# Attention with its causal masks on VectorE and GpSimd instead of TensorE, and two key steps per group

## What is computed

```
q, k, v = (h @ Wqkv + bqkv) split, 16 heads of 32, 1024 positions, 4 batches
scores = q k / sqrt(32), by key and query; masked where key > query (-10000)
attn = softmax(scores over the keys)
x = x + ga * ((attn applied to v) @ Wo + bo)
```

## Time and profile before

| | |
|---|---|
| median of 3 runs | 2444.23 us (2442.47 to 2448.04) |
| span of the profiled execution | 2451.0 us |
| TensorE busy | 2043.9 us (83%) |
| VectorE busy | 1115.6 us (46%) |
| ScalarE busy | 763.2 us (31%) |
| GpSimd busy | 510.1 us (21%) |
| attention, all four batches | about 60 to 1490 us |

### The profile page before, as it was taken

How to read it: one execution, slowest core, us unless ns; L and a number is a source line. 1 busy time by engine, 2 the same in 40 slices (tenths; PEclk the granted TensorE clock), 3 DMA queues, 4 the chain that set the end, 5 groups by cost and what they waited for, 6 DMA issues and landing times. The chain is left out here.

```text
span 2451.0 us, 34688 instructions
## 1 busy us (share of the span) xinstructions
PE 2043.9 (83%) x10812; PEld 1248.9 (51%) x10813; DVE 1115.6 (46%) x2207; ACT 763.2 (31%) x1215; POOL 510.1 (21%) x491
## 2 busy tenths in 40 slices
PE   4899997899987889987998995899999939999900
PEld 1644543654444545434544532676776726666600
DVE  3434553354444345443444435555665323333358
ACT  1244452344452244452244442122221102222200
POOL 0200005100006000006000014444555421000064
PEclk8899998899998899998899997999999969999955
DMA  6212213211213221213222114222222168333388
GB/s 215 52 27 52 44 44 105 52 38 41 52 35 105 52 52 37 42 35 104 52 52 52 32 41 182 71 93 82 90 90 95 65 231 282 127 127 128 116 280 320
DMA packets 104965, 232.49 MB, mean 95 GB/s; under 512 B 20440, under 2 KB 20440, under 8 KB 104812
## 3 DMA queue, kind: packets, MB, share of 16 engines
q1 hardware_dynamic: 81008, 171.86, 24.4%
q0 software_dynamic: 14848, 50.34, 5.7%
q10 hardware_dynamic: 8960, 8.41, 1.2%
HBM read 113.06 MB, written 67.17 MB: 74 GB/s over the span
## 5 line engine op out<-in xcount | busy, mean ns | idle before, releaser
L459 DVE TENSOR_REDUCE mx<-ring 128x1 f32<-128x512 f32 (+3 forms) x640 | 369.4, 632 | 395.6 <-PE ring L569 305.0
L367 ACT ACTIVATE pr<-sc 128x1024 f32<-128x1024 f32 (+3 forms) x384 | 307.9, 810 | 416.3 <-PE sc L601 343.2
L617 PE MATMUL O<-pr,V 128*32 128x512 f32 (+3 forms) x3072 | 343.0, 524 | 34.7 <-ACT pr L367 29.5
L598 PE MATMUL sc<-stk 128*128 128x512 f32 (+3 forms) x768 | 271.0, 427 | 42.4 <-ACT stk L356 42.4
L598 PEld LDWEIGHTS sc<-stk 128*128 128x128 f32 x768 | 144.2, 200 | 292.2 <-issue 189.4
L322 POOL TENSOR_TENSOR oT<-oV,oD 128x512 f32<-128x512 f32 x32 | 41.0, 1282 | 1165.8 <-DVE oD L481 1165.8
L569 PE MATMUL ring<-stk 96*128 96x512 f32 (+3 forms) x768 | 258.7, 434 | 27.4 <-DMA stk<-st 26.9
L569 PEld LDWEIGHTS ring<-stk 96*128 96x128 f32 x768 | 154.8, 215 | 38.8 <-issue 16.4
L1475 PE MATMUL ue<-wu_e,xT_e 128*128 x632 | 151.2, 383 | 0.1
L1489 PE MATMUL de<-wd_e,aT_e 128*128 x316 | 148.5, 593 | 0.0
L481 DVE RECIPROCAL oD<-oD 128x512 f32<-128x512 f32 x32 | 105.5, 3330 | 88.5 <-ACT oD L379 88.5
(11 more groups left out here) (233 smaller groups left out, 3478.3 us busy)
## 6 DMA issues: line engine op xcount, KB each, us to landing
stk<-st SPq DMA_DIRECT2D x192, 256.0 KB, 5.0
x_e<-xs SPq DMA_DIRECT2D x79, 256.0 KB, 2.6
ys<-y_e SPq DMA_DIRECT2D x79, 256.0 KB, 2.0
oT<-in_L_attn_x_dram ACTq DMA_DIRECT2D x16, 512.0 KB, 5.7
xr<-in_L_attn_x_dram SPq DMA_DIRECT2D x32, 256.0 KB, 2.8
x1d<-h SPq DMA_DIRECT2D x32, 256.0 KB, 2.0
xb<-x1d SPq DMA_DIRECT2D x32, 256.0 KB, 3.1
part<-y_sh SPq DMA_DIRECT2D x32, 256.0 KB, 2.0
```

The lines of the kernel that those rows point to most:

```text
L367: nc.scalar.activation(pr[:, g % 3, :, off:], sc[g % 2][:, :, off:], ACT.Exp, scale=SCALE).then_inc(exp_done, 1)
L459: nc.vector.tensor_reduce(mx[:, heads[0]:heads[-1] + 1, qt, part], bank[:, 0:len(heads) * w].rearrange("p (e k) -> p e k", e=len(heads)), ...
L598: last = nc.tensor.matmul(sc[g % 2][:, e, off:], K.stk[:, p % 2, 1, e, i * P:(i + 1) * P], K.stk[:, p % 2, 0, e, c * CH + off:(c + 1) * CH ...
L617: last = nc.tensor.matmul(O[row:row + 32, off:], V[:, col:col + DH], pr[:, g % 3, e, off:], start=(i == 0), stop=(i == 4 * c + 3))
```

## The change

It takes both mask matmuls off TensorE. For the maxima, VectorE's `tensor_tensor_reduce` adds a mask (0 or -1e30, `K.mask`, 128 x 512 of f32, of which the last columns are used) to the product, writes the sum back to PSUM and reduces it by maximum; it takes one head at a time, so that 16 such instructions replace 12 of the 20 reductions of a pair, and 8 stay. For the scores the exponentials above the diagonal are set to zero by an `affine_select` on GpSimd (`upper_off`, two heads of 128 columns at once, 8 per pair), for which the weighted sums of these steps then wait.

The key steps run in six groups of two. `M_GROUP` gives the maxima tasks before, between and after the two scores of each group. The weighted sums of a group come together after the scores of the next one; those of steps 10 and 11 come after `m_transpose` of the next pair. There are four buffers `pr`. On ScalarE the copy of the second chunk comes after `mt_evac`. On VectorE both reciprocals of a head group come in the next even pair, after that pair's first reduction, and the POOL multiplications follow in the same pair. SyncE starts the DMAs of `stk` at the end of the scores of the pair two before, not of its weighted sums, and `ga_bc`, `gabo_bc` and `xr` share memory with `st` and are loaded after the last `stk`. The set-up ends with a clearing of its semaphores and a barrier of all engines, and makes fewer constants.

The core of the diff:

```diff
...
-M_FROM, M_RATE = 4, 3
+    nc.clear_and_free_semaphores(held)
+    nc.all_engine_barrier()
...
+M_GROUP = ((0, 0, 1), (2, 2, 1), (2, 2, 1), (2, 2, 1), (2, 2, 0), (0, 0, 0))
+PRB = 4
...
+
+        late = st[:, 0:2, :].bitcast(f32).rearrange("p a s -> p (a s)")
+        ga_bc, gabo_bc = late[:, 0:D], late[:, D:2 * D]
+        xr = late[:, 2 * D:4 * D].rearrange("p (j d) -> p j d", d=D)
         V, S_t = K.V, K.S
...
         mhi = sb("mhi", [P, NT, 2], f32r)
-        pr = sb("pr", [P, 3, 2, CH])
+        pr = sb("pr", [P, PRB, 2, CH])
...
             with sp.Fori(0, NB) as b:
-                sp.wait_ge(u_ready, b * NT + PRIMED)
-                sp.dma_start(ga_bc[:, :], K.modd[bass.ds(b, 1), GA, :].broadcast_to([P, D])).then_inc(mod2_in, 16)
-                sp.wait_ge(x1_ready, b * NT + PRIMED)
-                sp.dma_start(gabo_bc[:, :], K.modd[bass.ds(b, 1), GABO, :].broadcast_to([P, D])).then_inc(mod2_in, 16)
                 for p in range(NPAIR):
                     if p >= 2:
-                        sp.wait_ge(pv_done, b * (NPAIR * NST) + NST * (p - 1) + PRIMED)
+                        sp.wait_ge(sc_done, b * (NPAIR * NST) + NST * (p - 1))
                         apart(sp)
...
                                 .then_inc(stk_in[p % 2], 16)
+                for s in range(2):
+                    sp.wait_ge(stk_in[s], (b * NHG + NHG) * STACKED + PRIMED)
+                sp.dma_start(ga_bc[:, :], K.modd[bass.ds(b, 1), GA, :].broadcast_to([P, D])).then_inc(mod2_in, 16)
+                sp.dma_start(gabo_bc[:, :], K.modd[bass.ds(b, 1), GABO, :].broadcast_to([P, D])).then_inc(mod2_in, 16)
                 for j in range(NT):
-                    if j < 2:
-                        sp.wait_ge(x1_ready, b * NT + PRIMED)
-                    else:
+                    if j >= 2:
                         sp.wait_ge(x1_ready, b * NT + j - 1 + PRIMED)
...
+
+            def upper_off(b, p, s):
+
+                c, i = STEPS[s]
+                off = i * P - c * CH
+                g = p * NST + s
+                pool.wait_ge(exp_done, b * NPAIR * NST + g + 1 + PRIMED)
+                apart(pool)
+                t = pr[:, g % PRB, :, off:off + P]
+                nc.gpsimd.affine_select(out=t, in_=t, compare_op=ALU.is_ge, fill=0.0, base=0,
+                                        pattern=[[0, 2], [1, P]], channel_multiplier=-1).then_inc(tri_done, 1)
+
+            def normalise(b, n):
+                hg, c = n // 2, CHUNKS[n % 2]
+                pool.wait_ge(o_rec, b * 8 + n + 1)
+                nc.gpsimd.tensor_tensor(oT[:, hg, c * CH:(c + 1) * CH], oV[:, c, :], oD[:, c, :], ALU.mult).then_inc(o_norm, 1)
...
                 split_low(b, NT - 1)
-                for n in range(2 * NHG):
-                    hg, c = n // 2, CHUNKS[n % 2]
-                    pool.wait_ge(o_rec, b * 8 + n + 1)
-                    nc.gpsimd.tensor_tensor(oT[:, hg, c * CH:(c + 1) * CH], oV[:, c, :], oD[:, c, :], ALU.mult).then_inc(o_norm, 1)
+                for p in range(NPAIR):
+                    for s in DIAG:
+                        upper_off(b, p, s)
+                        if p % 2 == 0 and p >= 2 and s in (DIAG[1], DIAG[3]):
+                            normalise(b, p - 2 + DIAG.index(s) // 2)
+                    if p == NPAIR - 1:
+                        normalise(b, p - 1)
+                        normalise(b, p)
                 pool.wait_ge(mod2_in, b * 32 + 32)
...
-                if p >= 2:
-                    act.wait_ge(pv_done, b * NPAIR * NST + NST * (p - 1) + PRIMED)
...
                 act.wait_ge(sc_done, b * NPAIR * NST + g + 1)
-                if g >= 3:
-                    act.wait_ge(pv_done, b * NPAIR * NST + g - 2 + PRIMED)
-                nc.scalar.activation(pr[:, g % 3, :, off:], sc[g % 2][:, :, off:], ACT.Exp, scale=SCALE).then_inc(exp_done, 1)
+                if g >= PRB:
+                    act.wait_ge(pv_done, b * NPAIR * NST + g - PRB + 1 + PRIMED)
+                nc.scalar.activation(pr[:, g % PRB, :, off:], sc[g % 2][:, :, off:], ACT.Exp, scale=SCALE).then_inc(exp_done, 1)
...
                         exp(b, p, s)
-                        if s == TURN:
+                        if s == TURN + 1:
                             o_copy(b, 2 * p)
-                    o_copy(b, 2 * p + 1)
                     if p % 2 == 0 and p + 2 < NPAIR:
...
                         mt_evac(b, p + 1)
+                    o_copy(b, 2 * p + 1)
...
                 dve.wait_ge(m_done, b * NPAIR * NM + p * NM + n + 1)
-                nc.vector.tensor_reduce(mx[:, heads[0]:heads[-1] + 1, qt, part],
-                                        bank[:, 0:len(heads) * w].rearrange("p (e k) -> p e k", e=len(heads)),
-                                        AX.X, ALU.max).then_inc(m_red, 1)
+                if k0 <= qt * P < k0 + w:
+                    apart(dve)
+                    for x_, e in enumerate(heads):
+                        o = bank[:, x_ * w:(x_ + 1) * w]
+                        last = nc.vector.tensor_tensor_reduce(out=o, in0=o, in1=K.mask[:, CH - w:CH], scale=1.0, scalar=MASKED,
+                                                              op0=ALU.add, op1=ALU.max, accum_out=mx[:, e, qt, part:part + 1])
+                    last.then_inc(m_red, 1)
+                else:
+                    nc.vector.tensor_reduce(mx[:, heads[0]:heads[-1] + 1, qt, part],
+                                            bank[:, 0:len(heads) * w].rearrange("p (e k) -> p e k", e=len(heads)),
+                                            AX.X, ALU.max).then_inc(m_red, 1)
...
                 for p in range(NPAIR):
-                    n = 0
-                    for s in range(NST + 1):
-                        if p + 1 < NPAIR:
-                            while n < M_DUE[s]:
-                                m_reduce(b, p + 1, n)
-                                n += 1
-                        if s == TURN + 1 and p == NPAIR - 1:
-                            o_recip(b, p - 1)
                     if p + 1 < NPAIR:
+                        for n in range(NM):
+                            m_reduce(b, p + 1, n)
+                            if n == sum(M_GROUP[0]) - 1 and p % 2 == 0 and p >= 2:
+                                o_recip(b, p - 2)
+                                o_recip(b, p - 1)
                         m_rows(b, p + 1)
...
                         p_low(b, (p + 2) // 2)
-                    if p % 2:
-                        if p < NPAIR - 1:
-                            o_recip(b, p - 1)
-                        o_recip(b, p)
+                o_recip(b, NPAIR - 2)
+                o_recip(b, NPAIR - 1)
                 dve.wait_ge(mod2_in, b * 32 + 32)
...
                 bank = bank_for(b, "m", NM * p + n)
-                diag = k0 <= qt * P < k0 + w
                 for x_, e in enumerate(heads):
-                    o = bank[:, x_ * w:(x_ + 1) * w]
-                    last = nc.tensor.matmul(o, K.stk[0:96, p % 2, 0, e, qt * P:(qt + 1) * P], K.stk[0:96, p % 2, 1, e, k0:k0 + w],
-                                            start=True, stop=not diag)
-                    if diag:
-                        last = nc.tensor.matmul(o[:, qt * P - k0:qt * P - k0 + P], K.identb[:, :], K.mask_qk[:, :],
-                                                start=False, stop=True)
+                    last = nc.tensor.matmul(bank[:, x_ * w:(x_ + 1) * w], K.stk[0:96, p % 2, 0, e, qt * P:(qt + 1) * P],
+                                            K.stk[0:96, p % 2, 1, e, k0:k0 + w], start=True, stop=True)
                 last.then_inc(m_done, 1)
...
                 pe.wait_ge(mt_ready, b * 16 + 2 * p + CHUNKS.index(c) + 1)
-                diag = i * P >= c * CH
                 for e in range(2):
                     last = nc.tensor.matmul(sc[g % 2][:, e, off:], K.stk[:, p % 2, 1, e, i * P:(i + 1) * P],
-                                            K.stk[:, p % 2, 0, e, c * CH + off:(c + 1) * CH], start=True, stop=not diag)
-                    if diag:
-                        last = nc.tensor.matmul(sc[g % 2][:, e, off:off + P], K.identb[:, :], K.mask_kq[:, :], start=False, stop=True)
+                                            K.stk[:, p % 2, 0, e, c * CH + off:(c + 1) * CH], start=True, stop=True)
                 last.then_inc(sc_done, 1)
...
                     pe.wait_ge(o_copied, b * 16 + n + PRIMED)
-                pe.wait_ge(exp_done, b * NPAIR * NST + g + 1 + PRIMED)
+                if s in DIAG:
+                    pe.wait_ge(tri_done, b * NPAIR * ND + p * ND + DIAG.index(s) + 1)
+                else:
+                    pe.wait_ge(exp_done, b * NPAIR * NST + g + 1 + PRIMED)
                 for e in range(2):
...
                         row = 64 * z + 32 * e
-                        last = nc.tensor.matmul(O[row:row + 32, off:], V[:, col:col + DH], pr[:, g % 3, e, off:],
+                        last = nc.tensor.matmul(O[row:row + 32, off:], V[:, col:col + DH], pr[:, g % PRB, e, off:],
```

(32 more changed lines are left out.)

36 lines of the change are left out of this document (18 added, 18 removed).

## The result

The changed kernel takes 2542.99 us (median of 4 runs, 2540.82 to 2545.02), the kernel before in the same set 2443.35 us: a ratio of 1.0402, 95% interval 1.0378 to 1.0425. That is 100 us slower. Forecast were 2525 us, 81 slower, in a range of 2420 to 2600. The profiled execution has a span of 2539.1 us against 2451.0, 88 us more: the profiled execution of the kernel before is longer than its median, that of the changed one shorter.

The account below looks back on a forecast made before the run. TensorE's in-order list was taken to set the length. A batch: +3.0 - 5.3 + 3 x 1.7 + 3 x 6.15 - 1.3 = +20.0 us; four batches and the barrier +81, so 2525 us, range 2420 to 2600.

Parts of the forecast that it names:

- The first wait: TensorE's first maxima matmul of a pair waits for the DMAs into stk: 8.3 us in odd, 5 in even pairs.
- The second: In pairs 2, 4 and 6 TensorE's task 4 waits 7.1 us for a ring bank while VectorE does both reciprocals.
- an odd pair: Length of an odd pair, with the wait for stk and 2.0 us for the clock: 31.0 us against 29.3, +1.7.
- an even pair: Length of an even pair from 2 on, without projection, with both waits: 33.85 us against 27.7, +6.15.
- pair 7: Last pair of a batch, with no maxima to prepare: about 21.7 us against 23.0, -1.3.
- TensorE's own list: TensorE's work and short waits from a pair's first maxima task to the next m_transpose: 17.3 us, with maxima matmuls 4.5.
- x: Extra time of each tensor_tensor_reduce on VectorE for handing over its scalar result: 0 to 0.168 us, taken as 0.1.
- Rival A: VectorE becomes the bound because the new instruction runs at half rate or its result costs much: about 2620 us; chance 0.1.
- The clock: Idling of 7 to 8 us drops TensorE to 1.2 GHz: 2.0 us for each of six pairs a batch.
- B: The reciprocals' wait doesn't hurt, so 7.1 us drop out of 12 pairs: 2440 us; chance 0.14.
- C: Neither wait stands, the copies land before they are asked for: about 2250 us, or 2350 with half the waits; chance 0.1.
- D: The masks' matmuls were hidden, so TensorE's list is 3.4 us longer in each pair: about 2630 us; chance 0.04.

Follow-up runs that it names:

- late tasks: Changed kernel with later M_GROUP, first maxima task behind scores 2, 3 and weighted sums 0, 1: 1.0097 alone, 0.9715 with reciprocals before the pair's first maximum.
- the projection first: Changed kernel with reciprocals before the first maximum and the next projection moved from the end of even pairs to behind scores 0 and 1: 0.9713; 0.9519 with later M_GROUP.
- the wait filled: Changed kernel with reciprocals before the first maximum, plus matmuls nobody reads (34 in odd, 17 in even pairs from 2) in TensorE's wait for stk: 2426.68 us, 0.9905.
- masks back: Changed kernel with its new order kept but both masks again matmuls on TensorE, plain reductions and no select: 2619.04 us, 1.0686.
- the kernel with the reciprocals first: Changed kernel with VectorE's two reciprocals before instead of after the first maximum in even pairs from 2 on: 2457.89 us, 1.0009.

## Why the prediction was right, point by point

**The first wait** was forecast as 8.3 us in odd pairs and 5 in even ones, from the 10.0 us of the copy and what is left to do meanwhile. Measured: 8.26 and 4.51, and from `m_transpose` to the landing 11.67 us (157.00 to 168.67) where I had 11.7. That this wait costs what it seems to is shown by the kernels with late tasks and with the projection first: the loss goes when something else covers the copy or starts it earlier.

**The second** was forecast as 7.1 us, with TensorE at task 4 again 8.55 us after the landing. It got there 8.50 us after it (205.15 - 196.65). The bare wait was 5.67, less than 7.1, because the work of 1.4 us ahead of it ran at half clock and took 2.8 (8.50 less 5.67). Moving the reciprocals took 96 us away.

**The terms of a batch**, in us against the means of before in the table:

| term | forecast | measured |
|---|---|---|
| maxima of pair 0 | +3.0 | 0.0 |
| pair 0 | -5.3 | -4.2 |
| an odd pair | +1.7 | +2.1 |
| an even pair | +6.15 | +7.5 to 7.8 |
| pair 7 | -1.3 | -0.5 |

With three odd and three even pairs the measured terms give +24.5, four times that 98, where the medians are 100 apart. The two profiled spans are only 88 apart, since the part behind the attention, which nothing changed, took 9.6 us less in the changed kernel's profile. Two sums of the prediction don't come out of its own figures. 24 masks at 0.13 us and 8 at half of that are 3.6 us and not 3.4. For pair 0, 40.2 less 48 x 0.23 is 29.2 and not 28; with the length in the trace, 39.2, it is 28.2, and the term would be -5.6. The deviations:

- *TensorE's own list.* I had 17.3 us from the first maxima task to the next `m_transpose`. With the wait filled, so at full clock, it is 18.9 us (170.49 to 189.39), 1.6 more; the changed kernel takes 20.3 (168.67 to 188.98), so the half clock is 1.4 of it, where I had 2.0. The mis-sized term is the maxima's matmuls: 24 of them and what stands between them take 6.4 us there and not 4.5; scores 2 to 11 take 3.9 (I had 3.6) and weighted sums 0 to 9 7.8 (8.4). Little of that is the price of narrow matmuls: I scaled them by columns to 0.13 and 0.12 us, and four of them (two of 256, two of 128 columns) take 0.62 us (184.38 to 185.00 above), 0.155 each, so 0.2 us for the eight. The larger part is gaps at the ring. In the same kernel, from 170 us to the next `m_transpose`, TensorE's weight loads wait for VectorE's reductions (us in total, times, longest):

```profile
PEld ring L592 <- DVE mx L485: 1.8, 3, 0.8
PEld ring L592 <- DVE mx L489: 1.8, 4, 0.8
```

These 3.6 us lie in part under matmuls that still run. The prediction put waits for VectorE behind the start at nothing.

The masks I had at 3.4 us a pair. Measured are 2.2 us (changed against masks back: 2.1, 2.6, 2.0 and 1.9 by kind of pair).
- *VectorE.* I took 0.1 us for the handing over of the scalar. Groups by shape of the changed kernel, 130 to 400 us:

```profile
L485 DVE CUSTOM_DVE_ANT_0 ring<-ring,mask 128x512 f32<-128x512 f32 x26 | 17.8, 716 | 0.9 <-PE ring L592 0.9
L485 DVE DVE_READ_ACCUMULATOR2_ANT mx<- 128x1 f32 x110 | 15.6, 142 | 0.0
L485 DVE CUSTOM_DVE_ANT_0 ring<-ring,mask 128x128 f32<-128x128 f32 x28 | 7.8, 321 | 0.0
```

The read of the accumulator is an instruction of its own, 142 ns, but starts within the tail of the main one, as the next main one does: two reductions of 128x512 start 0.60 to 0.65 us apart, plain ones 0.60. So x was near zero. The 20 tasks of pair 0 take VectorE 12.0 us (109.2 to 121.2) against 12.1 before, where I had summed whole durations to 13.0 and added 1.6 for x. The Trainium skill ("VectorE: DVE Perf Modes", Two Vector instructions with no wait between them) counts two instructions, and the trace agrees: 110 of the second, 142 ns each. Rival A is out as the bound: in the odd pairs TensorE's waits for VectorE are single ones of up to 0.8 us.
- *Pair 7.* I followed its list to a start of the output product 1.3 us earlier. VectorE and TensorE in the changed kernel:

```profile
400.95 3.35 DVE L511 RECIPROCAL oD<-oD 128x512 f32<-128x512 f32 x1 [21.10 <-ACT oD L401]
...
405.80 1.53 PE L646 MATMUL ring<-wo_sb,oT 128*128 128x512 f32 x3 [2.39 <-POOL oT L325]
```

The reciprocal of the first chunk starts at 400.95, 19.2 us into the pair, and GpSimd's multiplication keeps TensorE waiting 2.39 us for the output product. The pair takes 24.05 us, so the step "about 21.7" was too short by 2.3. Most of that is the clock, for which I had no term in this pair. Pair 7 in the second batch of the kernel before, and in the first of the kernel with the reciprocals first, whose lists for this pair are those of the changed kernel:

```profile
713.75:738.66 24.91, 20.12 (x149) 8.06 (x145) 3.35 (x1) 15.11 (x22) 1.27 (x1) 0.93 0.00 1
...
361.92:384.44 22.52, 16.53 (x148) 7.62 (x145) 4.45 (x2) 14.88 (x22) 4.44 (x9) 1.00 0.00 1
```

The changed kernel has 0.93 and 24.05 us in the same pair, and nearly so in every batch; at 1.00 the same lists take 22.52, 1.5 less. The kernel before takes 23.35 at 1.00 and 24.9 at 0.93. So by like clocks the pair is 0.8 us shorter, not 1.3. What decides whether the clock falls here stays open.
- *GpSimd.* A select over two heads took 0.41 us (mean 409 ns on the page), at the lower end of the bounds, and from 130 to 400 us TensorE's weight loads wait for it 14 times, 8.2 us in all, but no matmul of pairs 0 to 6 is shown waiting for it. Costed at nothing: that fits there. The longer of these waits come where TensorE waits 0.8 us for ScalarE's copy at the same time; a kernel that separates the two was not run.
- *The clock.* Four stretches of one us of the changed kernel, behind the wait of pair 1 and behind the second of pair 2:

```profile
172.00:173.00 1.00, 1.00 (x4) 0.48 (x2) 1.00 (x3) 0.32 (x2) 0.00 (x0) 0.56 0.02 8
173.00:174.00 1.00, 1.00 (x13) 0.31 (x16) 0.74 (x2) 0.94 (x1) 0.00 (x0) 1.00 0.00 0
209.00:210.00 1.00, 1.00 (x12) 0.06 (x4) 0.00 (x0) 0.00 (x0) 0.00 (x0) 0.50 0.00 0
210.00:211.00 1.00, 1.00 (x6) 0.40 (x3) 0.00 (x0) 0.00 (x0) 0.00 (x0) 0.79 0.00 0
```

At 172 the clock is still 0.56 and at 173 it is 1.00: 4.2 us of dense work at half speed in pair 1. In pair 2 the two waits join into one stretch at half clock that ends in the stretch at 210, and the work from 205.15 on falls into it. The Trainium skill ("TensorE: Matmul & The Clock Gate", Part 1) says that activity releases the clock; by that rule the filled wait keeps it, and the trace agrees, 1.00 throughout. The prediction saw the same rule in the first maxima stage. That row bears out the lower level only: TensorE is busy for 12.45 of 13.00 us there, and the clock stays at 0.50.

**Rivals B and C** (no second wait, no wait) did not happen; the kernel with the reciprocals first is B made real, 1.0009 where B's price was 2440 of 2444, 0.998. **D** (the masks' matmuls come back as nothing) is out by the two pairs of kernels with and without them.

So of the 19 us between 81 and 100, by the table, even pairs are 17 (list and a longer half clock), odd pairs 5, pair 0 4 and pair 7 3, and the maxima of pair 0, which cost nothing more, take 12 off: 18 in all, the rest is rounding. The two waits were right in place and nearly in size, but the total is as close as it is because misses of 30 us and of 12 us the other way offset each other in part. The barrier's 1 us is shown by no run.

## What to carry to other kernels

Work taken off the busiest engine pays only from the point where that engine doesn't wait; before moving steps into groups, list for each wait in the engine's list what stands ahead of it, how long its DMA or its releaser takes, and what covered that so far. Here a 10 us copy lost its cover and two reciprocals were put ahead of the release of a bank, and that cost 6.9% against the 2.8% that the masks brought. A wait that can't be shortened should be met by independent work (here the next projection, which also starts the next copy earlier), and that also keeps the clock up (1.00 in pair 2 of that kernel, 0.85 in the changed one).

## What was not expected

- Adding the mask and reducing in one VectorE operation costs no more than reducing: 716 ns against 686 at 512 columns, with its 142 ns read overlapped.
- A select on GpSimd over 2 x 128 columns takes 0.41 us, as long as one over 128 in the set-up. The shapes differ (two heads by a step, one row), so that is no rule for its rate.
- Filling the waits with matmuls that nobody reads made the kernel 1.0% faster.
- TensorE's 128- and 256-column matmuls with new weights of 96 x 128 each come 0.155 us apart, so below 256 columns fewer columns bring little.
- The granted clock of a stretch that no edit touched can differ: pair 7 is 22.5 us at 1.00 and 24.05 at 0.93 with the same lists. A single batch would have misled by that much.
